# Graph network on one core: node addition, exponentials and node-row copy of two convolutions in units of 1024 columns

## The chip, the core and the metric

The kernel runs on one core of a Trainium2 chip. The metric is the device time of one execution in microseconds (us); lower is better.

## What is computed

Four graph layers follow one another over 50,000 nodes of 128 features and 25,000 edges sorted by destination. Layer 1 holds the two convolutions that are changed here. Cut to one of them (8 heads of 16 channels):

```python
q = (x @ qw + qb).reshape(N, HEADS, CH)      # k and v alike
alpha = jnp.sum(q[dst] * k[src], axis=-1) * SCALE
m = jax.ops.segment_max(alpha, dst, num_segments=N)
a = jnp.exp(alpha - m[dst])
denom = jax.ops.segment_sum(a, dst, num_segments=N)
a = a / denom[dst]
msg = v[src] * a[:, :, None]
out = jax.ops.segment_sum(msg, dst, num_segments=N).reshape(N, HEADS * CH)
return out + x @ sw + sb
```

The first convolution is followed by a relu, the second by the addition of x and a layer norm.

## The kernel before

The work is cut into 49 tiles. A tile is 512 edges and 1024 node rows. Tables lie in HBM: each node has a row, and each run of edges with one destination leaves its result in an edge row; a later layer gathers from both. In `conv` (line 773) features lie on the partitions while edges run along the free dimension.

One step of the loop handles tile `now`, finishes tile `last` (one before) and, in the first convolution, stores what `old` (two before) left. The order on each engine is written out by hand in the four `step` functions; each engine runs its own order, and semaphores alone join them. The loop `run_steps` (line 75) writes out 6 steps, runs a hardware loop of 6 steps a turn, and writes out the rest.

- POOL gathers 4 x 128 source rows and 4 x 128 destination rows a tile (line 765), two tiles of buffers.
- SP loads the 1024 node rows of the tile and stores results.
- TensorE turns source rows (`turn(0)`), destination rows (`turn(1)`), multiplies q, turns both halves of the node rows (`turn(2)`, `turn(3)`), multiplies k and v, then `own_rows(now, 0)` (node rows times the self weight), in the second convolution `own_rows(now, 1)` too, then the sum over heads into `psA`. In the first convolution `own_rows(now, 1)` stands after `psA`. Last come 16 matmuls for the edge rows of `last` into `psE[2]`.
- ScalarE copies the turned rows out of PSUM (lines 946 and 975), keeps q, takes the exponentials `c` of `dropm` and `p` of `u` (lines 960 and 964), and the logarithm and exponential that invert the denominator. In the first convolution it applies the relu to edge and node rows; in the second it makes squares (line 954) and scales rows (line 931).
- VectorE runs the chain over the edges: running maximum `m` (line 1023), `drop`, `u`, `dropm`, then with the exponentials `pv` and the scans `den` and `num`, then `kq` of the current tile, `agg` of the last, and the node addition: line 1077 in the first convolution (adds a bias row), line 1009 in the second (`add_x1`, adds a prepared row). The reduction of squares `c_var` (line 444) stands between `dropm` and `pv` in the second.

PSUM is full: `psT` two banks, `psQ`, `psV`, `psA` one each, `psE` three (two for node rows, one for edge rows). The semaphore `en_ready` counts finished halves of node rows, `pren_ready` their additions, `turned_sb` the copies of turned rows (four a tile).

Of the kernel before, what the change touches and what calls it, by code (L numbers as in the profile page):

```python
# [768 lines left out]
def conv(nc, io, h, layer):  # L769
# [3 lines left out]
    with ExitStack() as ctx:  # L773
# [17 lines left out]
        drop, dropm, c, u, p = (sb(n, [P, TILE]) for n in ("drop", "dropm", "c", "u", "p"))  # L791
# [7 lines left out]
        psT = [bank(f"psT{k}") for k in range(2)]  # L799
        psQ, psV, psA = bank("psQ"), bank("psV"), bank("psA")  # L800
        psE = [bank(f"psE{k}") for k in range(3)]
# [5 lines left out]
         drop_ready, dropm_ready, c_ready, u_ready, p_ready, pv_ready, den_ready, num_ready, lnd_ready, rden_ready,  # L807
# [3 lines left out]
             "carry_ready", "m_ready", "drop_ready", "dropm_ready", "c_ready", "u_ready", "p_ready", "pv_ready",  # L811
# [12 lines left out]
        @block.sync  # L824
        def _(sp):
            def step(t):
                now, last, (g, a, b) = t.tile(0), t.tile(1), t.group(2)
                if now:
                    s = now.slot
                    wait(sp, turned, 4 * now.n - 4)  # L830
                    sp.dma_start(xn[:, s, :, :], node_rows(table, now.n)).then_inc(node_landed[s], 16)
                    if not layer:
                        here = bass.ds(now.n * TILE, TILE)
                        wait(sp, m_ready, now.n - 1)
                        sp.dma_start(h.far[:, here], io["far"][:, here].to_broadcast([P, TILE])
                                     ).then_inc(far_landed[s], 16)
                if layer:

                    u0 = t.group(0)[0]
                    if u0:  # L840

                        wait(sp, pren_ready, 2 * u0.n - 2)
                        sp.sem_inc(starts_sp, 1)
                        wait(sp, pree_ready, u0.n - 2)
                        sp.sem_inc(starts_sp, 1)
                    if now:
                        sp.dma_start(x1r[:, u0.slot, 0:2, :], node_rows(io["x1b"], now.n)).then_inc(x1n_landed[now.slot], 16)
                    if last:
                        sp.dma_start(by_row(x1r[:, u0.slot, 2, :]),
                                     edge_rows(io["x1"], last.n)).then_inc(x1e_landed[last.slot], 16)  # L850
                if layer:
                    store_group(sp, g, a, b, t, result, xo, out_ready, node_stored, edge_stored)
                    return
                if last:
                    sp.wait_ge(out_ready, last.n + 1)
                    sp.dma_start(node_rows(result, last.n), xo[:, last.slot, 0:2, :]).then_inc(node_stored[last.slot], 16)
                old = t.tile(3)
                if old:
                    sp.wait_ge(oute_ready, old.n + 1)
                    sp.dma_start(edge_rows(result, old.n), by_row(xe[:, old.slot, :])).then_inc(edge_stored[old.slot], 16)  # L860

            run_steps(sp, 3, step)
            all_stored(sp, node_stored, edge_stored)

        @block.tensor
        def _(pe):
            def turn(k, now, rows, landed, count):
                pe.wait_ge(landed, count)
                wait(pe, turned_sb, 4 * now.n + k - 1)
                for o, x in zip(quarters(psT[k % 2]), quarters(rows)):  # L870
                    ins = nc.tensor.transpose(o, x, h.w["ident"][:, :])
                ins.then_inc(turned, 1)

            def own_rows(now, k):

                pe.wait_ge(turned_sb, 4 * now.n + 3 + k)
                wait(pe, pren_ready, 2 * now.n - 1 + k)
                for o, x in zip(quarters(psE[k]), quarters(xnT[:, now.slot, k, :])):
                    ins = nc.tensor.matmul(o, x, w_s[:, :], start=True, stop=True)
                ins.then_inc(en_ready, 1)  # L880

            def step(t):
                now, last = t.tile(0), t.tile(1)
                if now:
# [3 lines left out]
                    pe.wait_ge(turned_sb, 4 * now.n + 2)  # L888
# [17 lines left out]
                if last:  # L906
# [3 lines left out]
                    for o, x, y in zip(quarters(psE[2]), quarters(agg), quarters(xdT[:, last.slot, :])):  # L910
# [7 lines left out]
        def _(act):  # L918
# [17 lines left out]
            def step(t):  # L936
                now, last, old, (g, a, b) = t.tile(0), t.tile(1), t.tile(2), t.group(1)
                if now:
                    s = now.slot
                    for k, dst in enumerate((xsT[:, s, :], xdT[:, s, :])):  # L940
# [5 lines left out]
                        nc.scalar.activation(dst, psT[k][:, :], ACT.Copy).then_inc(turned_sb, 1)  # L946
                if layer and g:

                    if a == 0:
                        act.wait_ge(pren_ready, 2 * g.n + 2)  # L950
# [6 lines left out]
                if last:  # L957
                    act.wait_ge(dropm_ready, last.n + 1)
                    wait(act, num_ready, last.n)
                    nc.scalar.activation(c[:, :], dropm[:, :], ACT.Exp).then_inc(c_ready, 1)  # L960
                    act.wait_ge(u_ready, last.n + 1)
                    wait(act, pv_ready, last.n)
                    wait(act, den_ready, last.n)
                    nc.scalar.activation(p[:, :], u[:, :], ACT.Exp).then_inc(p_ready, 1)
                if old and not layer:
                    act.wait_ge(ee_ready, old.n + 1)
                    wait(act, edge_stored[old.slot], 16 * old.half)
                    nc.scalar.activation(xe[:, old.slot, :], psE[2][:, :], ACT.Relu).then_inc(oute_ready, 1)
# [21 lines left out]
                if now and not layer:  # L990
                    act.wait_ge(pren_ready, 2 * now.n + 2)
# [6 lines left out]
        def _(dve):  # L998
            nc.vector.memset(m[:, 0, 0:1], 0.0).then_inc(carry_ready, 1)

            def add_x1(t, g, k):
                now, old = t.tile(0), t.tile(2)
                if k < 2:
                    dve.wait_ge(en_ready, 2 * now.n + 1 + k)
                    dve.wait_ge(x1n_landed[now.slot], 16 * (now.half + 1))
                else:
                    dve.wait_ge(ee_ready, old.n + 1)
                    dve.wait_ge(x1e_landed[old.slot], 16 * (old.half + 1))
                nc.vector.tensor_tensor(pre[:, g.slot, k, :], psE[k][:, :], x1r[:, g.slot, k, :],
                                        ALU.add).then_inc(pren_ready if k < 2 else pree_ready, 1)  # L1010

            def step(t):
# [12 lines left out]
                if layer and b == 3:  # L1025
                    add_x1(t, g, 2)
                if last:
# [4 lines left out]
                    wait(dve, p_ready, last.n)  # L1032
                    nc.vector.tensor_tensor(u[:, :], psA[:, :], m[:, s, 1:TILE + 1], ALU.subtract).then_inc(u_ready, 1)
                    dve.wait_ge(drop_ready, last.n + 1)
                    wait(dve, c_ready, last.n)
# [6 lines left out]
                if last:  # L1042

                    dve.wait_ge(p_ready, last.n + 1)
# [4 lines left out]
                    dve.wait_ge(c_ready, last.n + 1)  # L1049
# [22 lines left out]
                if now and not layer:  # L1072

                    wait(dve, out_ready, now.n - 1)
                    for k in range(2):
                        dve.wait_ge(en_ready, 2 * now.n + 1 + k)
                        nc.vector.tensor_tensor(by_row(pre[:, now.slot, k, :]), by_row(psE[k][:, :]),  # L1077
                                                s_bias[:, :].rearrange("p (o f) -> p o f", o=1).to_broadcast([P, 4, P]),
                                                ALU.add).then_inc(pren_ready, 1)
                if layer:  # L1080
# [4 lines left out]
                    for k in range(a0, min(b0, 2)):  # L1085
                        add_x1(t, g0, k)
# [816 lines left out]
```

## Time and profile before

| | us |
|---|---|
| median of 3 runs | 3386.93 |
| lowest, highest | 3383.4, 3388.3 |
| the profiled execution | 3391.02 |
| its span in the trace | 3389.2 |
| VectorE busy | 2556.6 (75%) |
| TensorE busy (matmuls) | 2705.1 (80%) |
| ScalarE busy | 2020.4 (60%) |
| POOL busy | 2088.8 (62%) |

The span is the trace's own time from first to last instruction. Busy shares are means over stages with different limits. The stages that count here are the first convolution (about 681 to 1243 us) and the second (about 1245 to 1826 us). In the rows further down an idle time in brackets is that of the engine just before the instruction, with what ended it. Tiles carry a prefix in the trace: `c_` is either convolution. `c_psE` there is any of the three banks, and `s_b` and `x1r` are what the node addition adds.

### The profile page before, as it was taken

How to read it: one execution, taken by the hardware profiler on the slowest of the kernel's cores; microseconds unless marked ns; L12 is line 12 of the kernel's file. 1: busy time of each engine (PE TensorE's matmuls, PEld its weight loads, DVE VectorE, ACT ScalarE, POOL GpSimd, SP SyncE). 2: the span in 40 equal slices, each digit the busy share in tenths (PEclk: the TensorE clock that was granted, in tenths of full speed). 3: DMA queues.
4: the chain of work that ended last, by engine and by line, in shares of the span. 5: the costliest groups of instructions: out<-in, count | busy, mean ns of one | idle time of the engine just before them, and what ended most of it. 6: DMA issues, size and time to landing. Idle time of an engine off the chain costs nothing. (4 is left out here: it accounts for less than half of the span.)

```text
span 3389.2 us, 49347 instructions
## 1 busy us (share of the span) xinstructions
PE 2705.1 (80%) x14422; PEld 1818.1 (54%) x14422; DVE 2556.6 (75%) x2973; ACT 2020.4 (60%) x3316; POOL 2088.8 (62%) x1966
## 2 busy tenths in 40 slices
PE   7899999778888868888886899999999875444442
PEld 3466666556666645656563356666666554323221
DVE  6699999958888859999995269989989997323332
ACT  0167777545665548898985577787787775111111
POOL 4477777377777747777773764555554000777776
PEclk9999999989999989999997999999999997666666
DMA  6366676645555547776763266666666563322221
GB/s 204 112 195 218 221 222 219 197 152 179 185 181 177 178 145 225 228 234 226 235 225 113 56 170 183 182 194 182 184 187 191 163 194 126 88 71 75 77 82 40
DMA packets 447965, 569.11 MB, mean 168 GB/s; under 512 B 60559, under 2 KB 253255, under 8 KB 447682
## 3 DMA queue, kind: packets, MB, share of 16 engines
q1 hardware_dynamic: 379758, 441.14, 42.1%
q0 software_dynamic: 62720, 124.71, 13.4%
q10 hardware_dynamic: 5332, 1.32, 0.2%
q8 instruction: 82, 1.34, 0.2%
q14 instruction: 73, 0.60, 0.1%
HBM read 350.28 MB, written 220.55 MB: 168 GB/s over the span
## 5 line engine op out<-in xcount | busy, mean ns | idle before, releaser
L1176 POOL DMA_INDIRECT g_xd_xs<-table_x,dst_row x196 | 230.7, 1177 | 315.9 <-PE g_psT L1241 222.1
L1673 POOL DMA_INDIRECT f_xs<-table_x,src_row x196 | 188.6, 962 | 314.9 <-POOLq L1100 255.5
L765 POOL DMA_INDIRECT c_xs<-table_h,src_row x196 | 215.0, 1097 | 121.0 <-issue 75.9
L506 POOL DMA_INDIRECT xs<-in_x,src_i x196 | 227.4, 1160 | 84.9 <-issue 55.2
L491 POOL DMA_INDIRECT xd<-in_x,dst_i x196 | 217.0, 1107 | 96.6 <-issue 47.2
L1722 PE MATMUL f_psT<-w_ident,f_xs 128*128 128x128 f32 x196 | 53.0, 424 | 277.9 <-DMA f_xs<-table_x,src_row 277.9
L765 POOL DMA_INDIRECT c_xs<-table_x,src_row x196 | 201.6, 1029 | 116.5 <-issue 62.4
L1736 ACT ACTIVATE f_reluT<-f_psY 128x512 f32<-128x512 f32 x49 | 29.3, 597 | 403.9 <-PE f_psY L1715 403.9
L1176 POOL DMA_INDIRECT g_xd_xs<-table_x,src_row x196 | 221.8, 1132 | 59.7 <-issue 59.4
L765 POOL DMA_INDIRECT c_xd<-table_x,dst_row x196 | 204.7, 1044 | 59.7 <-issue 59.7
L1782 DVE TENSOR_TENSOR_SCAN f_red<-f_cont,f_red,f_psT 128x512 f32<-128x512 uint8 x48 | 61.4, 1280 | 226.9 <-PE f_psT L1722 226.8
L1680 POOL DMA_INDIRECT out<-f_xo,end_i x196 | 195.6, 998 | 59.7 <-issue 59.1
L765 POOL DMA_INDIRECT c_xd<-table_h,dst_row x196 | 185.8, 948 | 59.7 <-issue 59.7
L1722 PEld LDWEIGHTS f_psT<-w_ident,f_xs 128*128 128x128 f32 x196 | 34.3, 212 | 344.7 <-DMA f_xs<-table_x,src_row 343.0
L1246 PE MATMUL g_psP<-w_center,g_turns 128*128 128x128 f32 x1568 | 196.8, 279 | 17.4 <-ACT g_turns L1376 11.2
L1246 PEld LDWEIGHTS g_psP<-w_center,g_turns 128*128 128x128 f32 x1568 | 186.9, 194 | 36.2 <-ACT g_turns L1376 14.5
L1463 DVE TENSOR_REDUCE g_var<-g_sq 128x12 f32<-128x1536 f32 x98 | 171.6, 1751 | 25.2 <-ACT g_sq L1420 22.7
L931 ACT ACTIVATE c_xo<-c_pre,c_rstd 128x128 f32<-128x128 f32 x588 | 181.9, 388 | 5.5 <-ACT c_rstd L456 4.8
L890 PE MATMUL c_psQ<-c_xdT,w_q 128*128 128x512 f32 x196 | 112.9, 658 | 74.6 <-ACT c_xdT L946 74.6
L993 ACT ACTIVATE c_xo<-c_pre 128x1024 f32<-128x1024 f32 x49 | 51.9, 1058 | 166.8 <-DVE c_pre L1077 166.8
L894 PE MATMUL c_psQ<-c_xsT,w_k 128*128 128x512 f32 x196 | 111.3, 650 | 36.1 <-ACT c_q L924 36.1
L896 PE MATMUL c_psV<-c_xsT,w_v 128*128 128x512 f32 x196 | 105.1, 618 | 36.3 <-DVE c_pv L1046 36.3
(313 smaller groups left out, 8689.2 us busy)
## 6 DMA issues: line engine op xcount, KB each, us to landing
g_share<-shares SPq DMA_DIRECT2D x196, 192.0 KB
xn<-in_x SPq DMA_DIRECT2D x49, 512.0 KB
table_x<-xo SPq DMA_DIRECT2D x49, 512.0 KB, 3.0
table_x1b<-xb SPq DMA_DIRECT2D x49, 512.0 KB, 5.4
c_xn<-table_x SPq DMA_DIRECT2D x49, 512.0 KB
table_h<-c_xo SPq DMA_DIRECT2D x49, 512.0 KB
c_xn<-table_h SPq DMA_DIRECT2D x49, 512.0 KB
c_x1r<-table_x1b SPq DMA_DIRECT2D x49, 512.0 KB
```

The lines of the kernel that those rows point to most:

```text
L491: pool.indirect_dma_start(out=quarters(h.xd0[:, s, :])[j], out_offset=None, in_=io["x0"], in_offset=edge_index(h.dst_i, n, j)).then_inc(h. ...
L506: pool.indirect_dma_start(out=quarters(h.xs0[:, s, :])[j], out_offset=None, in_=io["x0"], in_offset=edge_index(h.src_i, n, j)).then_inc(h. ...
L765: pool.indirect_dma_start(out=quarters(rows[:, s, :])[j], out_offset=None, in_=table, in_offset=edge_index(columns, now.n, j)).then_inc(la ...
L890: nc.tensor.matmul(psQ[:, :], w_q[:, :], xdT[:, s, :], start=True, stop=True).then_inc(q_ready, 1)
L894: nc.tensor.matmul(psQ[:, :], w_k[:, :], xsT[:, s, :], start=True, stop=True).then_inc(k_ready, 1)
L896: nc.tensor.matmul(psV[:, :], w_v[:, :], xsT[:, s, :], start=True, stop=True).then_inc(v_ready, 1)
L931: ins = nc.scalar.activation(quarters(xo[:, g.slot, j // 4, :])[j % 4], quarters(pre[:, g.slot, j // 4, :])[j % 4], ACT.Copy, scale=rstd[: ...
L1176: pool.indirect_dma_start(out=quarters(xd_xs[:, s, k, :])[j], out_offset=None, in_=table, in_offset=edge_index(columns, now.n, j)).then_in ...
L1246: ins = nc.tensor.matmul(o, x, h.w["center"][:, :], start=True, stop=True)
L1463: nc.vector.tensor_reduce(var[:, :], by_row(sq[:, :, :].rearrange("p b n -> p (b n)")), AX_X, ALU.add).then_inc(ready, 1)
L1673: pool.indirect_dma_start(out=quarters(xs[:, s, :])[j], out_offset=None, in_=table, in_offset=edge_index(h.src_row, now.n, j)).then_inc(sr ...
L1680: pool.indirect_dma_start(out=io["out"], out_offset=edge_index(h.end_i, old.n, j), in_=quarters(xo[:, s, :])[j], in_offset=None, bounds_ch ...
```

## The change

`dropm` and `u` become the two halves of one buffer `args`, `c` and `p` those of `exps`; one exponential of 1024 columns is taken of the whole buffer once both are there. The two banks of `psT` become one tensor of two banks, and one copy moves both halves of the turned node rows. The node rows get a pair of banks `psN` of their own, with `psE` left as the one bank for edge rows; one addition of 1024 columns handles both halves and waits for the second half's matmuls. `en_ready` and `pren_ready` count once a tile, and `turned_sb` three times. The order of instructions on every engine stays otherwise as it was.

```diff
-        drop, dropm, c, u, p = (sb(n, [P, TILE]) for n in ("drop", "dropm", "c", "u", "p"))
+        drop, args, exps = sb("drop", [P, TILE]), sb("args", [P, 2, TILE]), sb("exps", [P, 2, TILE])
+        (dropm, u), (c, p) = ((x[:, 0, :], x[:, 1, :]) for x in (args, exps))
...
-        psT = [bank(f"psT{k}") for k in range(2)]
+        pair = lambda name: ctx.enter_context(nc.psum_tensor(tag + name, [P, 2, TILE], F32))
+        psT, psN = pair("psT"), pair("psN")
         psQ, psV, psA = bank("psQ"), bank("psV"), bank("psA")
-        psE = [bank(f"psE{k}") for k in range(3)]
+        psE = bank("psE")
...
         def _(pe):
             def turn(k, now, rows, landed, count):
                 pe.wait_ge(landed, count)
-                wait(pe, turned_sb, 4 * now.n + k - 1)
-                for o, x in zip(quarters(psT[k % 2]), quarters(rows)):
+                wait(pe, turned_sb, 3 * now.n + max(k - 1, 0))
+                for o, x in zip(quarters(psT[:, k % 2, :]), quarters(rows)):
                     ins = nc.tensor.transpose(o, x, h.w["ident"][:, :])
                 ins.then_inc(turned, 1)
 
             def own_rows(now, k):
 
-                pe.wait_ge(turned_sb, 4 * now.n + 3 + k)
-                wait(pe, pren_ready, 2 * now.n - 1 + k)
-                for o, x in zip(quarters(psE[k]), quarters(xnT[:, now.slot, k, :])):
+                pe.wait_ge(turned_sb, 3 * now.n + 3)
+                wait(pe, pren_ready, now.n)
+                for o, x in zip(quarters(psN[:, k, :]), quarters(xnT[:, now.slot, k, :])):
                     ins = nc.tensor.matmul(o, x, w_s[:, :], start=True, stop=True)
-                ins.then_inc(en_ready, 1)
+                if k == 1:
+                    ins.then_inc(en_ready, 1)
...
                 if last:
                     act.wait_ge(dropm_ready, last.n + 1)
+                    act.wait_ge(u_ready, last.n + 1)
                     wait(act, num_ready, last.n)
-                    nc.scalar.activation(c[:, :], dropm[:, :], ACT.Exp).then_inc(c_ready, 1)
-                    act.wait_ge(u_ready, last.n + 1)
                     wait(act, pv_ready, last.n)
                     wait(act, den_ready, last.n)
-                    nc.scalar.activation(p[:, :], u[:, :], ACT.Exp).then_inc(p_ready, 1)
+                    nc.scalar.activation(exps[:, :, :], args[:, :, :], ACT.Exp).then_inc(exps_ready, 1)
...
                 if now:
                     if not layer:
                         keep_q(now)
-                    for k in range(2):
-                        act.wait_ge(turned, 4 * now.n + k + 3)
-                        wait(act, en_ready, 2 * now.n - 3 + k)
-                        nc.scalar.activation(xnT[:, s, k, :], psT[k][:, :], ACT.Copy).then_inc(turned_sb, 1)
+                    act.wait_ge(turned, 4 * now.n + 4)
+                    wait(act, en_ready, now.n - 1)
+                    nc.scalar.activation(xnT[:, s, :, :], psT[:, :, :], ACT.Copy).then_inc(turned_sb, 1)
...
-            def add_x1(t, g, k):
-                now, old = t.tile(0), t.tile(2)
-                if k < 2:
-                    dve.wait_ge(en_ready, 2 * now.n + 1 + k)
-                    dve.wait_ge(x1n_landed[now.slot], 16 * (now.half + 1))
-                else:
-                    dve.wait_ge(ee_ready, old.n + 1)
-                    dve.wait_ge(x1e_landed[old.slot], 16 * (old.half + 1))
-                nc.vector.tensor_tensor(pre[:, g.slot, k, :], psE[k][:, :], x1r[:, g.slot, k, :],
-                                        ALU.add).then_inc(pren_ready if k < 2 else pree_ready, 1)
+            def add_nodes(now, g):
+                dve.wait_ge(en_ready, now.n + 1)
+                dve.wait_ge(x1n_landed[now.slot], 16 * (now.half + 1))
+                nc.vector.tensor_tensor(pre[:, g.slot, 0:2, :], psN[:, :, :], x1r[:, g.slot, 0:2, :],
+                                        ALU.add).then_inc(pren_ready, 1)
+
+            def add_edges(old, g):
+                dve.wait_ge(ee_ready, old.n + 1)
+                dve.wait_ge(x1e_landed[old.slot], 16 * (old.half + 1))
+                nc.vector.tensor_tensor(pre[:, g.slot, 2, :], psE[:, :], x1r[:, g.slot, 2, :],
+                                        ALU.add).then_inc(pree_ready, 1)
...
                 if now and not layer:
 
                     wait(dve, out_ready, now.n - 1)
-                    for k in range(2):
-                        dve.wait_ge(en_ready, 2 * now.n + 1 + k)
-                        nc.vector.tensor_tensor(by_row(pre[:, now.slot, k, :]), by_row(psE[k][:, :]),
-                                                s_bias[:, :].rearrange("p (o f) -> p o f", o=1).to_broadcast([P, 4, P]),
-                                                ALU.add).then_inc(pren_ready, 1)
+                    dve.wait_ge(en_ready, now.n + 1)
+                    nc.vector.tensor_tensor(by_row(pre[:, now.slot, 0:2, :].rearrange("p b n -> p (b n)")),
+                                            by_row(psN[:, :, :].rearrange("p b n -> p (b n)")),
+                                            s_bias[:, :].rearrange("p (o f) -> p o f", o=1).to_broadcast([P, 8, P]),
+                                            ALU.add).then_inc(pren_ready, 1)
                 if layer:
 
                     g0, a0, b0 = t.group(0)
                     if g0:
                         wait(dve, out_ready, g0.n - 1)
-                    for k in range(a0, min(b0, 2)):
-                        add_x1(t, g0, k)
+                    if g0 and a0 == 0:
+                        add_nodes(now, g0)
```

What is left out renames the same counts and buffers elsewhere (for example `wait(sp, pren_ready, 2 * u0.n - 2)` becomes `u0.n - 1`).

## Rows read from the trace of the kernel before

**Rows 1.** Windows of both convolutions: length, PE, PEld, DVE, ACT, POOL busy, PEclk, DMA.

```profile
720.00:1230.00 510.00, 439.55 (x2614) 323.26 (x2614) 412.01 (x560) 305.70 (x512) 376.79 (x362) 1.00 0.57 177
1280.00:1800.00 520.00, 446.71 (x2555) 312.10 (x2556) 501.49 (x641) 467.40 (x1098) 374.69 (x365) 1.00 0.72 230
```

**Rows 2.** Waits, 680 to 1245 us: waiting work, what ended it, us, times, longest.

```profile
DVE c_pv L1046 <- ACT c_p L964: 56.5, 49, 1.2
...
DVE c_pre L1077 <- PE c_psE L879: 45.9, 50, 1.1
...
PE c_psT L871 <- DMA c_xs<-table_x,src_row: 21.7, 1, 21.7
```

**Rows 3.** Timeline, one step of the first convolution: start us, us, engine, line, operation.

```profile
1010.00 1.27 DVE L1023 TENSOR_TENSOR_SCAN c_m<-far,c_m,c_psA 128x512 f32<-128x512 f32 x1
...
1011.61 0.60 ACT L946 ACTIVATE c_xsT<-c_psT 128x512 f32<-128x512 f32 x1 [0.36 <-PE c_psT L871]
...
1013.23 0.63 ACT L960 ACTIVATE c_c<-c_dropm 128x512 f32<-128x512 f32 x1 [0.53 <-DVE c_dropm L1036]
...
1013.77 0.61 ACT L964 ACTIVATE c_p<-c_u 128x512 f32<-128x512 f32 x1
...
1014.42 0.75 DVE L1046 SCALAR_TENSOR_TENSOR c_pv<-c_psV,b_vs,c_p 128x512 f32<-128x512 f32 x1 [1.15 <-ACT c_p L964]
...
1015.33 1.08 ACT L975 ACTIVATE c_xnT<-c_psT 128x512 f32<-128x512 f32 x2
...
1015.50 1.13 PE L894 MATMUL c_psQ<-c_xsT,w_k 128*128 128x512 f32 x2 [0.74 <-ACT c_q L924]
...
1017.32 1.05 PE L879 MATMUL c_psE<-w_s,c_xnT 128*128 128x128 f32 x8
...
1018.24 1.13 PE L903 MATMUL c_psA<-c_kq,w_heads 128*128 128x512 f32 x2
...
1018.69 0.69 DVE L1077 TENSOR_TENSOR c_pre<-c_psE,s_b 128x512 f32<-128x512 f32 x1
...
1019.20 1.05 PE L879 MATMUL c_psE<-w_s,c_xnT 128*128 128x128 f32 x8
...
1020.29 0.69 DVE L1077 TENSOR_TENSOR c_pre<-c_psE,s_b 128x512 f32<-128x512 f32 x1 [0.91 <-PE c_psE L879]
```

**Rows 4.** Tile c_pre, 670 to 1245 us: min, median, max ns, first and last start.

```profile
L1077 DVE TENSOR_TENSOR c_pre<-c_psE,s_b x98: 681/691/693, 701.7 to 1228.1; 128x512 f32<-128x512 f32 x98
```

**Rows 5.** Waits of the second convolution, 1250 to 1810 us.

```profile
DVE c_var L444 <- ACT c_sq L954: 18.0, 47, 0.4
```

**Rows 6.** Timeline, part of one step of the second convolution.

```profile
1503.48 1.28 DVE L1009 TENSOR_TENSOR c_pre<-c_psE,c_x1r 128x512 f32<-128x512 f32 x2
...
1503.94 0.38 PE L911 MATMUL c_psE<-w_center,c_agg 128*128 128x128 f32 x2
...
1506.37 0.60 ACT L946 ACTIVATE c_xsT<-c_psT 128x512 f32<-128x512 f32 x1 [0.90 <-PE c_psT L871]
...
1508.85 1.75 DVE L444 TENSOR_REDUCE c_var<-c_sq 128x12 f32<-128x1536 f32 x1 [0.37 <-ACT c_sq L954]
...
1509.80 0.64 ACT L964 ACTIVATE c_p<-c_u 128x512 f32<-128x512 f32 x1
...
1510.52 0.74 DVE L1046 SCALAR_TENSOR_TENSOR c_pv<-c_psV,b_vs,c_p 128x512 f32<-128x512 f32 x1
```

**Rows 7.** Groups by form, whole run, at 1024 columns: us, mean ns, idle before.

```profile
L750 DVE TENSOR_TENSOR xb<-xo,s_b1c 128x1024 f32<-128x1024 f32 x49 | 60.0, 1224 | 1.7
L1623 DVE TENSOR_TENSOR g_pre<-g_psP,g_xn 128x1024 f32<-128x1024 f32 x49 | 59.9, 1221 | 21.6 <-PE g_psP L1246 21.6
...
L993 ACT ACTIVATE c_xo<-c_pre 128x1024 f32<-128x1024 f32 x49 | 51.9, 1058 | 166.8 <-DVE c_pre L1077 166.8
...
L662 ACT ACTIVATE nodeT<-psT 128x1024 f32<-128x1024 f32 x49 | 49.8, 1016 | 3.8 <-PE psT L582 3.8
```

**Rows 8.** Line L765, gathers of the first convolution: min, median, max ns.

```profile
L765 POOL DMA_INDIRECT c_xs<-table_x,src_row x196: 940/944/1540, 681.3 to 1203.5; - x196
```

More of the change, by code:

```diff
@@ L840, in step @@
                     if u0:
-                        wait(sp, pren_ready, 2 * u0.n - 2)
+                        wait(sp, pren_ready, u0.n - 1)
                         sp.sem_inc(starts_sp, 1)
@@ L887, in step @@
                     turn(1, now, xd[:, s, :], dst_landed[s], 64 * (now.half + 1))
-                    pe.wait_ge(turned_sb, 4 * now.n + 2)
+                    pe.wait_ge(turned_sb, 3 * now.n + 2)
                     wait(pe, kq_ready, now.n)
@@ L909, in step @@
                     wait(pe, pree_ready if layer else oute_ready, last.n)
-                    for o, x, y in zip(quarters(psE[2]), quarters(agg), quarters(xdT[:, last.slot, :])):
+                    for o, x, y in zip(quarters(psE), quarters(agg), quarters(xdT[:, last.slot, :])):
                         nc.tensor.matmul(o, x, to_rows[:, :], start=True, stop=False)
@@ L945, in step @@
                             wait(act, ee_ready, now.n - 1)
-                        nc.scalar.activation(dst, psT[k][:, :], ACT.Copy).then_inc(turned_sb, 1)
+                        nc.scalar.activation(dst, psT[:, k, :], ACT.Copy).then_inc(turned_sb, 1)
                 if layer and g:
                     if a == 0:
-                        act.wait_ge(pren_ready, 2 * g.n + 2)
+                        act.wait_ge(pren_ready, g.n + 1)
                     if b == 3:
@@ L990, in step @@
                 if now and not layer:
-                    act.wait_ge(pren_ready, 2 * now.n + 2)
+                    act.wait_ge(pren_ready, now.n + 1)
                     wait(act, node_stored[s], 16 * now.half)
@@ L1025, in step @@
                 if layer and b == 3:
-                    add_x1(t, g, 2)
+                    add_edges(t.tile(2), g)
                 if last:
@@ L1031, in step @@
                                             ALU.subtract).then_inc(drop_ready, 1)
-                    wait(dve, p_ready, last.n)
+                    wait(dve, exps_ready, last.n)
                     nc.vector.tensor_tensor(u[:, :], psA[:, :], m[:, s, 1:TILE + 1], ALU.subtract).then_inc(u_ready, 1)
                     dve.wait_ge(drop_ready, last.n + 1)
-                    wait(dve, c_ready, last.n)
+                    wait(dve, exps_ready, last.n)
                     nc.vector.scalar_tensor_tensor(out=dropm[:, :], in0=drop[:, :], scalar=0.0, in1=h.far[:, here],
@@ L1042, in step @@
                 if last:
-                    dve.wait_ge(p_ready, last.n + 1)
+                    dve.wait_ge(exps_ready, last.n + 1)
                     wait(dve, num_ready, last.n)
```

8 lines of the change are left out of this document (4 added, 4 removed).

## The prediction

> **What bounds the kernel now.** The change touches the two convolutions only, so I read the stage windows first. Over 510 us of the first convolution and 520 us of the second TensorE holds its full granted clock (1.00). VectorE is busy 412 of 510 us (81%) in the first and 501 of 520 us (96%) in the second [rows 1]. In the first no engine is full, so a chain of waits must set the step; in the second VectorE looks like the bound and has to be checked for a wait that comes back in each step.
>
> Waits of the first convolution [rows 2]: VectorE waits 49 times for the second exponential (c_p, 56.5 us, 1.15 us each) and 50 times for the matmuls of the node rows (45.9 us, 0.92 us each). TensorE waited for gathered rows once (21.7 us, the fill). So neither gathers nor VectorE's own load sets the step.
>
> One step in time order [rows 3]: running maximum c_m at 1010.00; the first exponential starts at 1013.23, as soon as dropm is there (ScalarE idle 0.53 before it); the second at 1013.77; pv at 1014.42 after VectorE had waited 1.15; K on TensorE at 1015.50, which waited for q; own rows 0 at 1017.32; psA, which needs kq, at 1018.24; first half of the node addition at 1018.69; matmuls of the second half of the node rows at 1019.20 (TensorE goes straight on from psA to them); second half of the addition at 1020.29, after VectorE had waited 0.91. The next c_m stands behind this addition on VectorE. That closes the cycle: c_m, exponentials, pv, kq, psA, own rows 1, second addition, next c_m. Its length over the stage: the 98 additions start between 701.7 and 1228.1 [rows 4]; taking off the 1.60 from first to second half of one tile (1018.69 to 1020.29), 48 steps take 524.8 us, 10.93 each.
>
> The second convolution [rows 5, 6]: VectorE waits in 47 steps of 49 for the squares c_sq (18.0 us, 0.38 each). The cycle there is kq, psA, the edge rows on TensorE (1503.94 on), the turns of xs, c_xsT (1506.37, ScalarE idle 0.90 before it, until those turns), c_xdT, c_sq, c_var on VectorE (1508.85, idle 0.37 before it), pv, the scans, kq. The two node additions (1503.48, 1.28 us the pair) stand after agg and before c_m, which belongs to VectorE's other branch (c_m, drop, u, dropm): beside that cycle, not on it. That branch has 0.37 us of slack.
>
> **The change, part by part.**
>
> *Node addition, first convolution.* Removed: two instructions of 0.69 us [rows 4]. Added: one of 1024 columns. Two existing instructions bracket it: an addition of 1024 columns from two PSUM banks is 1.221 us, one with the same kind of 8-fold broadcast from SBUF is 1.224 us [rows 7]. I take 1.22. In time on the engine that saves 1.28 - 1.22 = 0.06. But the first half is not on the path: it runs at 1018.69 to 1019.38, in time that VectorE would otherwise spend waiting for the matmuls of 1019.20 [rows 3]. The new addition waits for both halves (en_ready is now raised only by the second), so all 1.22 us come after those matmuls instead of 0.69. Neighbours on VectorE overlap by about 0.1 (the pair of [rows 6] takes 1.28 for twice 0.69), which I take as the same behind a wide one, so c_m starts 1.22 - 0.69 = 0.53 us later. The cover that hid half one is given up. Per tile +0.53, 49 tiles: +26.0 us. What is queued behind the waiting addition is c_m of the next step and all of VectorE's chain; nothing there can go ahead. ScalarE's relu of the node rows, which already waited for both halves, also comes 0.5 later; behind it c_xsT had 0.36 of idle time and c had 0.53 against a c_m that moves as well [rows 3], so it starts nothing late. SP's store of those rows moves with it and has a step of time.
>
> *Exponential, first convolution.* The first one waits for dropm already, and u is made before dropm, so the single one starts when the first did. The pair takes 1013.23 to 1013.77 + 0.61 = 1.15 us. ScalarE's 1024-column relu from SBUF is 1.058 us [rows 7]. I take 1.06 for the exponential, so it saves 0.09. Bounds: 1.06 if it prices like the relu, and at most 1.15 if nothing overlapped away is gained; below 1.06 nothing is excluded by a row, and 1.02 is the price of the 1024-column copy from PSUM [rows 7]: a saving between 0 and 0.13. Both branches behind it (pv on VectorE; xe, q, K on TensorE) move by it together, so it is on the path: -0.09 x 49 = -4.4 us. Scan den needs c, which would be ready later than before, but den stands behind pv, which needs p: no loss.
>
> *Copy of turned node rows, first convolution.* The pair takes 1015.33 to 1016.41 (1.08); one copy of 1024 columns from two banks is 1.016 us [rows 3, 7]. Own rows 0 used to need the first copy only and now need the joint one, done by 1016.4. TensorE is at K and V from 1015.50 on and comes to own rows 0 at 1017.32 [rows 3]. So 0.9 us of cover is left: 0. If that cover were gone it would cost half a copy, 0.5 us a step. The turns of the next tile wait for the joint copy of this one, over at 1016.4; the c_xsT made from them starts at 1011.61 + 10.93 = 1022.5: 0.
>
> First convolution: +0.53 - 0.09 = +0.44 us a step (step 10.93 to 11.37), 49 steps: +21.6 us.
>
> *Second convolution.* Here both halves of own rows are done before psA, so the joint addition waits for nothing new. It saves 1.28 - 1.22 = 0.06 us of VectorE between agg and c_m. That lies beside the binding cycle, and the wait for c_sq grows from 0.37 to about 0.43: worth 0. The joint exponential and copy shorten ScalarE by 0.09 and 0.07, between q and lnv. Their consumer pv starts behind c_var on VectorE, and lnv behind c_var too: 0. Bounds: if the saving of the addition were on the path, -0.06 x 49 = -3 us; if the exponential's were as well, -7 us; p was over at 1509.80 + 0.64 = 1510.44 and pv started at 1510.52 behind c_var, so the exponential was just in time and comes 0.09 sooner now. I take 0.
>
> In the first convolution VectorE is 81% busy and half one runs beside own rows 1 [rows 1, 3]; in the second VectorE is 96% busy. The Trainium skill ("Perfetto Trace Analysis", Optimizing Scalar/DVE Operations) says that grouping helps a saturated engine, while for an unsaturated one that leaves bubbles on others "breaking up instructions may allow work to be completed sooner". By its first half the sum would be that of rival A, by its second a loss in the first convolution, as computed; the trace of the first stage agrees with the second half.
>
> **Sum.** The profiled execution took 3391.0 us, 3391.0 + 21.6 = 3412.6. It lies 4.1 above the median of the runs, 3386.9; a shift of the median by the same 21.6 gives 3408.5 us, which I predict. Own range of this case: the addition between 1.22 and 1.28 (what the pair takes now, start to end), the exponential's saving between 0 and 0.13, the second convolution between -7 and 0: 21.6 + 2.9 + 4.4 = 28.9 above, 21.6 - 2.0 - 7.4 = 12.2 below, so 3399.1 to 3415.8.
>
> **Rivals.**
>
> *A. VectorE's and ScalarE's own work is the bound, and fewer instructions win.* If own rows 1 were finished when agg ends, the joint addition would start at once and everything saved would count: 0.06 + 0.09 in both convolutions, 98 x 0.15 = -14.7 us, 3372.2 us. For it: VectorE is 96% busy in the second convolution. Against it: the wait of 0.91 for own rows 1 in all steps of the first. It decides there: as long as own rows 1 end more than 0.06 after half one could, the joint form loses. Chance 0.07.
>
> *B. The gathers pace the convolutions.* A gather of POOL takes 0.944 us at the median and up to 1.54 [rows 8], and POOL issues them with hardly any pause. If the step of 10.9 us were POOL's, the 0.44 would be taken out of waits and the time stays: 3387. Against it: TensorE waited for gathered rows only in the fill [rows 2], and 8 gathers at the median of 0.944 are 7.6 of the 10.9 us. Chance 0.05.
>
> *C. TensorE loses its clock.* The longer step thins TensorE's work in the first convolution from 86% [rows 1] to about 83%. If the grant fell to its lower level there, K, V, own rows 0, psA and own rows 1 (1015.50 to 1020.2, 4.7 us of each step) would take twice as long: for a tenth of the steps +23 us on top, 3432. Full clock held at 86% in both stages; the trace of before does not show these stages at 83%. Chance 0.05.
>
> *D. The change does not do what it says*, one joint instruction costing as much as two because the two banks are read apart: the addition would be 1.38, 0.16 x 49 = +7.8 us more, 3416. The 1024-column rows from two banks exclude it nearly [rows 7]. Chance 0.02, inside the range.
>
> **How the numbers follow.** Forecast 0.81; A 0.07, B 0.05, C 0.05, D 0.02. The range 3399 to 3417 holds the forecast and D, and leaves out A, B and C. A measurement of this kernel tells about 0.2% (6.8 us) from no change. Slower by more: forecast, C, D, with a little taken off for a forecast case that meets all of its lower bounds: 0.87. Same: B and that little, 0.06. Faster: A, 0.07.
>
> **What would show it.** In the first convolution one c_pre of 128x1024 x49 at about 1.22 us with 1.5 us of idle time before each (75 us in all, against 45.9), c_m starting 1.1 to 1.15 after it, the wait of pv down from 1.15 to 1.06, second additions 11.34 us apart, and the stage ending some 21 us later. In the second: steps still 11.35 apart and the wait for c_sq up from 0.37 to 0.43. The forecast is wrong if the joint addition starts before 10.2 us after c_m, if steps of the first convolution stay under 11.1 us, or if the second's become shorter by over 0.05.

## The result

| | us |
|---|---|
| before, median of 5 runs | 3386.93 (3383.4 to 3388.3) |
| changed, median of 5 runs | 3414.19 (3406.83 to 3415.38) |
| ratio | 1.0077, 95% interval 1.0066 to 1.0089 |
| changed, the profiled execution | 3406.83, span 3405.0 |

The change is slower by 27 us (22 to 30 by the interval). The profiled execution is the fastest of the five, so the loss is placed stage by stage from the two traces. The table gives the starts of the running maximum c_m of the first and last tile of each convolution, and what lies around them:

| stage | before | changed | difference |
|---|---|---|---|
| start to first c_m | 704.1 | 700.5 | -3.6 |
| first convolution, 48 steps | 524.6 | 547.3 | +22.7 |
| between | 38.6 | 38.8 | +0.2 |
| second convolution, 48 steps | 544.5 | 544.3 | -0.2 |
| last c_m to end | 1577.4 | 1574.1 | -3.3 |
| span | 3389.2 | 3405.0 | +15.8 |

In these two executions the change cost 22.7 us, all in the first convolution. The two outer stages together are 6.9 us shorter in the changed kernel's execution, so the spans differ by 15.8 us only. They vary by as much over the six profiles taken at this speed: the first c_m starts at 700.5 to 704.1 us, and the run ends 1573.9 to 1578.5 us after the last one. The other four executions of the changed kernel took 3413.56 to 3415.38 us. None of them was profiled, so it is likely but not shown that their further 7 us, and with them the gap between 22.7 and 27, lie in the outer stages. A kernel of the experiments has such a spread by itself: of five executions of `wide_add_only_2` three took 3409.63 to 3411.05 us and two 3418.46 and 3419.15 us.

### The profile page after: what moved, and what is told of

Its sections match the earlier page's. It is cut to its first block and busy times, and to the rows that moved or that the text cites. A ratio compares the mean times of both kernels' runs of the same rounds, so it can differ in the third digit from the quotient of the medians.

```text
span 3405.0 us, 48520 instructions
## 1 busy us (share of the span) xinstructions
PE 2696.7 (79%) x14422; PEld 1812.1 (53%) x14422; DVE 2547.6 (75%) x2875; ACT 2000.6 (59%) x3120; POOL 2059.6 (60%) x1966
## 5 line engine op out<-in xcount | busy, mean ns | idle before, releaser
L765 POOL DMA_INDIRECT c_xs<-table_x,src_row x196 | 192.6, 982 | 163.8 <-issue 56.2
L765 POOL DMA_INDIRECT c_xs<-table_h,src_row x196 | 215.3, 1099 | 124.4 <-issue 76.2
L506 POOL DMA_INDIRECT xs<-in_x,src_i x196 | 225.8, 1152 | 85.2 <-issue 55.5
L765 POOL DMA_INDIRECT c_xd<-table_h,dst_row x196 | 185.4, 946 | 59.7 <-issue 59.7
L765 POOL DMA_INDIRECT c_xd<-table_x,dst_row x196 | 185.1, 944 | 59.7 <-issue 59.7
L1248 PEld LDWEIGHTS g_psP<-w_center,g_turns 128*128 128x128 f32 x1568 | 184.8, 192 | 36.8 <-ACT g_turns L1378 15.8
L897 PE MATMUL c_psQ<-c_xsT,w_k 128*128 128x512 f32 x196 | 110.9, 648 | 55.5 <-ACT c_q L927 55.5
L966 ACT ACTIVATE c_exps<-c_args 128x1024 f32<-128x1024 f32 x98 | 103.9, 1061 | 52.6 <-DVE c_args L1038 52.5
```

Of the source, the lines that this page charges most:

```text
L506: pool.indirect_dma_start(out=quarters(h.xs0[:, s, :])[j], out_offset=None, in_=io["x0"], in_offset=edge_index(h.src_i, n, j)).then_inc(h. ...
L765: pool.indirect_dma_start(out=quarters(rows[:, s, :])[j], out_offset=None, in_=table, in_offset=edge_index(columns, now.n, j)).then_inc(la ...
L897: nc.tensor.matmul(psQ[:, :], w_k[:, :], xsT[:, s, :], start=True, stop=True).then_inc(k_ready, 1)
L966: nc.scalar.activation(exps[:, :, :], args[:, :, :], ACT.Exp).then_inc(exps_ready, 1)
L1248: ins = nc.tensor.matmul(o, x, h.w["center"][:, :], start=True, stop=True)
```

## The profile after

Waits of the changed kernel, 680 to 1270 us (waiting work, what ended it, us in total, times, longest), answering to [rows 2]:

```profile
DVE c_pre L1078 <- PE c_psN L881: 78.6, 49, 2.7
...
PE c_psQ L897 <- ACT c_q L927: 55.5, 48, 1.2
POOL c_xs L765 <- PE c_psT L873: 54.4, 34, 1.6
...
DVE c_pv L1048 <- ACT c_exps L966: 52.0, 49, 1.1
```

VectorE now waits 78.6 us for the own rows where it was 45.9, 1.60 a step, and 52.0 instead of 56.5 for the exponential. TensorE waits for q 1.2 us a step (55.5 us in all, 36.1 before): its work did not grow, the step did. POOL, which before ran without a pause, now waits 34 times until a buffer of gathered rows has been turned: with longer steps the gathers run into their buffers. So they do not set the changed kernel's step. That they did not set the step of 10.9 us before either is shown by `rows_early_2` below, where the same gathers keep up with steps of 10.42 us.

One step as in [rows 3], start us, us, engine, line, operation:

```profile
1005.98 1.05 PE L881 MATMUL c_psN<-w_s,c_xnT 128*128 128x128 f32 x8
...
1007.14 1.23 DVE L1078 TENSOR_TENSOR c_pre<-c_psN,s_b 128x1024 f32<-128x1024 f32 x1 [1.58 <-PE c_psN L881]
...
1008.28 1.27 DVE L1025 TENSOR_TENSOR_SCAN c_m<-far,c_m,c_psA 128x512 f32<-128x512 f32 x1
...
1011.51 1.06 ACT L966 ACTIVATE c_exps<-c_args 128x1024 f32<-128x1024 f32 x1 [1.08 <-DVE c_args L1038]
...
1012.60 0.75 DVE L1048 SCALAR_TENSOR_TENSOR c_pv<-c_psV,b_vs,c_exps 128x512 f32<-128x512 f32 x1 [1.06 <-ACT c_exps L966]
...
1013.69 1.12 PE L897 MATMUL c_psQ<-c_xsT,w_k 128*128 128x512 f32 x2 [1.21 <-ACT c_q L927]
...
1015.51 1.05 PE L881 MATMUL c_psN<-w_s,c_xnT 128*128 128x128 f32 x8
...
1016.42 1.13 PE L906 MATMUL c_psA<-c_kq,w_heads 128*128 128x512 f32 x2
...
1017.39 1.05 PE L881 MATMUL c_psN<-w_s,c_xnT 128*128 128x128 f32 x8
...
1018.55 1.23 DVE L1078 TENSOR_TENSOR c_pre<-c_psN,s_b 128x1024 f32<-128x1024 f32 x1 [1.58 <-PE c_psN L881]
...
1019.69 1.27 DVE L1025 TENSOR_TENSOR_SCAN c_m<-far,c_m,c_psA 128x512 f32<-128x512 f32 x1
```

From c_m to c_m are 11.41 us. Own rows 1 starts 9.11 after c_m (before 9.20: the exponential's gain). But c_m follows 2.30 us after the start of own rows 1 (1017.39 to 1019.69), where it was 1.09 to the second addition and 0.6 more. Half one, which ran beside own rows 1 at 1018.69 in [rows 3], is now in the 1.23 us at 1018.55, behind them.

The wide additions of both convolutions by tile (min, median, max ns), answering to [rows 4], and the exponential from the page:

```profile
L1078 DVE TENSOR_TENSOR c_pre<-c_psN,s_b x49: 1224/1225/1225, 699.3 to 1246.7; 128x1024 f32<-128x1024 f32 x49
L1005 DVE TENSOR_TENSOR c_pre<-c_psN,c_x1r x49: 1208/1217/1225, 1285.5 to 1829.8; 128x1024 f32<-128x1024 f32 x49
```

```profile
L966 ACT ACTIVATE c_exps<-c_args 128x1024 f32<-128x1024 f32 x98 | 103.9, 1061 | 52.6 <-DVE c_args L1038 52.5
```

1.225 and 1.061 us: the prices taken from [rows 7]. The second convolution: four more lines of the step of before in [rows 6], then a step of the changed kernel, then its waits:

```profile
1502.87 0.69 DVE L1071 TENSOR_TENSOR c_agg<-c_num,c_rden 128x512 f32<-128x512 f32 x1
...
1504.68 1.27 DVE L1023 TENSOR_TENSOR_SCAN c_m<-far,c_m,c_psA 128x512 f32<-128x512 f32 x1
...
1505.51 0.39 PE L912 MATMUL c_psE<-s1c,c_xdT 128*128 128x128 f32 x2
...
1505.93 0.69 DVE L1009 TENSOR_TENSOR c_pre<-c_psE,c_x1r 128x512 f32<-128x512 f32 x1
```

```profile
1522.02 0.68 DVE L1073 TENSOR_TENSOR c_agg<-c_num,c_rden 128x512 f32<-128x512 f32 x1
...
1522.62 1.22 DVE L1005 TENSOR_TENSOR c_pre<-c_psN,c_x1r 128x1024 f32<-128x1024 f32 x1
...
1523.75 1.27 DVE L1025 TENSOR_TENSOR_SCAN c_m<-far,c_m,c_psA 128x512 f32<-128x512 f32 x1
...
1524.68 0.39 PE L915 MATMUL c_psE<-s1c,c_xdT 128*128 128x128 f32 x2
...
1525.10 0.69 DVE L1011 TENSOR_TENSOR c_pre<-c_psE,c_x1r 128x512 f32<-128x512 f32 x1
...
1528.03 1.75 DVE L444 TENSOR_REDUCE c_var<-c_sq 128x12 f32<-128x1536 f32 x1 [0.38 <-ACT c_sq L957]
```

```profile
DVE c_var L444 <- ACT c_sq L957: 18.0, 47, 0.4
...
DVE c_pre L1011 <- PE c_psE L915: 1.3, 7, 0.2
```

c_m follows agg by 1.73 us instead of 1.81 (1.74 and 1.80 at the median of all steps), so the wide form saves 0.06 to 0.08. The edge addition behind c_m now starts 1.35 after it (before 1.25 here, 1.28 at the median). In both kernels it starts 0.03 us after the modelled end of TensorE's edge rows (1505.90 and 1525.07), and seven waits for them are on record in the changed kernel, none in the same steps before. So TensorE holds the edge addition, which starts as long after agg as before, 3.1 us. The wait for c_sq stays at 18.0 us in 47 steps.

## The experiments

Twelve runs on three chips. On two of them, called disturbed below (first eight runs), the kernels took 3736 to 3779 us, the one before 3745 and 3742, and steps of the first convolution ran from 10 to 17 us; on the third (last four, "at full clock") all was as in the first profiles. So of the first eight the shortest steps speak, and the times only roughly. Stages at full clock are compared with the first profile of before; no profile of before was taken beside these runs.

**Undo the wide addition in the first convolution alone.**

```diff
-                    dve.wait_ge(en_ready, now.n + 1)
-                    nc.vector.tensor_tensor(by_row(pre[:, now.slot, 0:2, :].rearrange("p b n -> p (b n)")),
...
+                    for k in range(2):
+                        dve.wait_ge(en_ready, 2 * now.n + 1 + k)
+                        nc.vector.tensor_tensor(by_row(pre[:, now.slot, k, :]), by_row(psN[:, k, :]),
...
```

> The changed kernel with the node addition of the first convolution taken apart again: two additions of 512 columns, each waiting for its own half of own rows; the joint exponential, the joint copy and the wide addition of the second convolution stay. Theory (the wide addition lies wholly behind own rows 1, where half of it used to be covered): the step of the first convolution falls from 11.40 to 10.81 us (10.90 of before less 0.09 of the exponential), the time is 4 us under before, 3383, and 31 under the changed kernel. Rival (the joint exponential or the joint copy holds the chain up): the step stays above 11.0 and the time above 3395. Rival (the pairing of PSUM banks itself costs): the same, above 3395, with the wait for own rows unchanged at 1.6 us.

> The changed kernel with the node addition of the first convolution in two again, a second time. On the chip of the first time transfers were slower and most steps had other waits; the undisturbed ones took 10.80 us. Theory: where transfers are as fast as in the profile of before, all steps take 10.81, and the time is 4 us under before, 3383. Rival (joint exponential or copy costs): not under before.

> The changed kernel with the node addition of the first convolution in two, a third time, for a chip on which TensorE keeps its full clock through the first convolution, as in the profiles of before and after. Theory: all steps there take 10.81 us and the time is 4 us under before (ratio 0.9988). Rival (the joint exponential or copy costs): ratio 1.002 or more. If the clock falls in spells again, only the shortest steps speak: 10.80.

First and second: 3744.3 and 3743.9 against 3745.3 and 3742.1 us of before, ratios 1.0012 (0.9992 to 1.0031) and 1.0003 (0.9987 to 1.0018), shortest steps 10.80. Third: 3381.2 against 3388.7, ratio 0.9981 (0.9971 to 0.9990), 7.6 us less where 4 were expected; first convolution 520.3 us, 4.3 less than before, median step 10.81. Own rows 1 and what follows, in that kernel:

```profile
1001.72 0.68 DVE L1079 TENSOR_TENSOR c_pre<-c_psN,s_b 128x512 f32<-128x512 f32 x1
...
1002.21 1.05 PE L881 MATMUL c_psN<-w_s,c_xnT 128*128 128x128 f32 x8
...
1003.31 0.69 DVE L1079 TENSOR_TENSOR c_pre<-c_psN,s_b 128x512 f32<-128x512 f32 x1 [0.91 <-PE c_psN L881]
...
1003.91 1.27 DVE L1025 TENSOR_TENSOR_SCAN c_m<-far,c_m,c_psA 128x512 f32<-128x512 f32 x1
```

Half one is back beside own rows 1, and c_m follows own rows 1 by 1.70 us instead of 2.30. All of the loss goes with the wide addition of the first convolution, and the rest of the change is a small gain. PSUM pairing costs nothing: psN is a pair here too.

**One edit at a time.** `exps_only` is the kernel before with the joint exponential; `wide_add_only` the changed kernel with exponential and copy in two:

```diff
-                    nc.scalar.activation(exps[:, :, :], args[:, :, :], ACT.Exp).then_inc(exps_ready, 1)
+                    nc.scalar.activation(c, dropm, ACT.Exp).then_inc(exps_ready, 1)
...
+                    nc.scalar.activation(p, u, ACT.Exp).then_inc(exps_ready, 1)
```

> The kernel before with the joint exponential alone. Theory: the exponential pair of 1.15 us becomes one of 1.06 on the path of the first convolution, step 10.90 to 10.81, time 4.3 us less, 3382.6; nothing in the second convolution, where pv stands behind c_var. Rival (scan den or q waits longer since c comes later): step 10.90 or more, time 3387 or more. Rival (ScalarE's work bounds the second convolution): its step falls from 11.35 to 11.26, time 9 us less, 3378.

> The changed kernel with exponential and copy taken apart again, so that the wide node addition (both convolutions) is the only edit. Theory: own rows 1 to c_m takes 2.30 instead of 1.70 us in the first convolution, step 10.90 to 11.50, 49 steps, time 29 us more than before, 3416; second convolution unchanged at 11.35. Rival (the joint copy is part of the loss, since own rows 0 wait for it): here the loss is smaller than in the changed kernel, under 24 us, 3410 or less.

> The wide node addition as the only edit, a second time. Its shortest steps were 11.50 us. Theory: at full clock all steps of the first convolution take 11.50, the time is 29 us over before (ratio 1.0085) and 4 over the changed kernel. If the clock falls in spells again: shortest steps 11.50, ratio near 1.010 as the first time.

The exponential alone: ratio 1.0016 (0.9998 to 1.0034) on a disturbed chip, shortest step 10.80 as the theory has it; its time at full clock was not measured. The wide addition alone: 1.0100 (1.0073 to 1.0126), then 1.0071 (1.0057 to 1.0085), 3411.1 against 3388.7 us, 22 us where 29 were expected. Its stage says otherwise: 551.7 us, 27.1 over before, median step 11.50. The medians take in what the outer stages do; the profiled execution is one of the two slower ones, and its span, 3416.6, is 27.4 over the 3389.2 of before. Its waits, 680 to 1245 us:

```profile
DVE c_pre L1080 <- PE c_psN L881: 76.9, 48, 2.7
...
DVE c_pv L1050 <- ACT c_exps L967: 54.2, 47, 1.2
```

Step 11.50 here, 11.40 with exponential and copy joined: 0.10 for these two, as 10.90 to 10.81 above.

**The changed kernel again.**

> The changed kernel unaltered, for a second profile and more times. The first convolution was 22.7 us longer than before in the first profile, the second 0.2 shorter, and the stages that the change does not touch 6.9 us shorter. Theory (the untouched stages differ from run to run): again 547 us for the first convolution, 544 for the second, and untouched stages 3 to 8 us longer than in the first profile, so that the time is near 3414. Rival (the change lengthens an untouched stage in most executions): the start of the first convolution or what follows the second is longer than in the profile of before by 3 us or more.

3770.7 against 3745.3 us, ratio 1.0079 (1.0054 to 1.0104), shortest steps 11.40. It ran on a disturbed chip, so its stages cannot be set beside the first profiles. Against the rival that the change lengthens an outer stage stand the profiles at full clock: with the wide addition these stages take together 2274.6 us (changed), 2281.8 (`wide_add_only_2`) and 2274.7 (`rows_early_2`), before 2281.5. Where the slower executions of the changed kernel spend their further 7 us stays open.

**Own rows 1 ahead of psA**, so that it isn't the last thing of a step:

```diff
-                    if layer:
-                        own_rows(now, 1)
+                    own_rows(now, 1)
...
-                    if not layer:
-                        own_rows(now, 1)
```

> The changed kernel with own rows 1 of the first convolution put ahead of psA on TensorE, as it stands in the second convolution. Theory (the wide addition costs only because it waits for own rows 1 as the last thing of the step): own rows 1 ends 0.9 us earlier after c_m, the wait of 1.58 us before the addition falls to about 0.6, undisturbed steps of the first convolution take 10.45 us instead of 11.40, and the time is some 22 us under before and 46 under the changed kernel. Rival (the wide form is slower in itself): steps stay over 10.9. Rival (psA, now 0.9 later, holds up c_m instead): the step is near 10.9, with VectorE waiting for c_psA.

> The changed kernel with own rows 1 ahead of psA in the first convolution, a second time. Shortest steps were 10.42 us. Theory at full clock: steps 10.42 or as near to it as the gathers allow (8 at 1.25 us and what VectorE holds up), time 17 to 23 us under before (ratio 0.994). Rival: the gathers hold the steps at 10.9, ratio 1.000. If the clock falls in spells again: ratio 1.000 as the first time.

> The kernel before with own rows 1 of the first convolution ahead of psA. Theory: half one of the addition follows agg without a wait, half two ends before psA does, and c_m waits for psA: steps of 10.3 us where undisturbed instead of 10.90, time 29 us under before. Rival (gathers set a floor of 10.9): the steps stay at 10.9 with TensorE waiting for gathered rows.

First: ratio 1.0007 (0.9988 to 1.0027), shortest step 10.42. Second, at full clock: 3361.3 against 3388.7 us, ratio 0.9924 (0.9910 to 0.9937), 27 us under before where 17 to 23 were expected; all steps but the first (9.86) 10.41 to 10.43. In that kernel:

```profile
1009.64 1.95 PE L881 MATMUL c_psN<-w_s,c_xnT 128*128 128x128 f32 x16
...
1010.41 0.68 DVE L1070 TENSOR_TENSOR c_agg<-c_num,c_rden 128x512 f32<-128x512 f32 x1
...
1011.42 1.02 PE L905 MATMUL c_psA<-c_kq,w_heads 128*128 128x512 f32 x2
1011.69 1.22 DVE L1075 TENSOR_TENSOR c_pre<-c_psN,s_b 128x1024 f32<-128x1024 f32 x1 [0.60 <-PE c_psN L881]
...
1012.83 1.27 DVE L1022 TENSOR_TENSOR_SCAN c_m<-far,c_m,c_psA 128x512 f32<-128x512 f32 x1
```

The same wide addition waits 0.6 us instead of 1.58. psA and the addition now run side by side, and c_m starts 1.41 us after psA, where it takes 1.39 when it waits for psA alone (`add_later_2` below): both are ready at nearly the same time. This beats both kernels; the gain is in the first convolution, 499.7 us against 524.6. TensorE waits for gathered rows only in the fill, so gathers don't set this step. The kernel before with the same move (ratio 0.9989, 0.9974 to 1.0004, disturbed chip) had two steps of 10.17 and 10.28, where the theory had 10.3, and no other under 10.8; the first is 0.25 under the wide form. Whether it is faster at full clock was not measured.

**The wide addition inside VectorE's wait for the exponential.** The addition of `last` goes between the copy of the carry and pv of the next step, its relu behind the reciprocal, its store a step later:

```diff
                     nc.vector.tensor_copy(m[:, 1 - s, 0:1], m[:, s, TILE:TILE + 1]).then_inc(carry_ready, 1)
+                if last and not layer:
+                    wait(dve, out_ready, last.n - 1)
+                    dve.wait_ge(en_ready, last.n + 1)
+                    nc.vector.tensor_tensor(by_row(pre[:, last.slot, 0:2, :].rearrange("p b n -> p (b n)")),
...
```

> The changed kernel with the wide node addition of the first convolution moved on VectorE from the end of a step to the next one, between the copy of the carry and pv, where VectorE waits 1.06 us for the exponential; the relu of the node rows follows the reciprocal on ScalarE, and SP stores them one step later, so that the next load is not queued behind the store. Theory (the addition is worth its time only where the engine waits anyway): c_m starts as soon as psA is there, undisturbed steps would be 9.5 us, and the gathers, 8 at 1.25 us, hold them at 10.0 to 10.4; time 24 to 44 us under before. Rival (the gathers, which VectorE holds up for 0.9 us a step, set 10.9): no better than the split addition. Rival (the addition delays pv by more than 0.1 us): steps over 10.4 with VectorE never waiting for the exponential.

> The changed kernel with the wide addition moved into VectorE's wait for the exponential, a second time. Shortest steps were 9.96 us, the pace of 8 gathers. Theory at full clock: steps of 10.0 to 10.4, time 24 to 44 us under before (ratio 0.987 to 0.993). Rival: the gathers, held up by VectorE, hold the steps at 10.9, ratio 1.000. If the clock falls in spells again: ratio 0.998 as the first time.

First: ratio 0.9984 (0.9969 to 1.0000). Second: 3367.9 against 3388.7 us, ratio 0.9936 (0.9922 to 0.9950); 21 us, a little short of the 24 to 44 expected; median step 10.44, from 9.20 (the first, with rows gathered ahead) to 12.56.

```profile
1003.79 1.28 DVE L1026 TENSOR_TENSOR_SCAN c_m<-far,c_m,c_psA 128x512 f32<-128x512 f32 x1 [0.85 <-PE c_psA L907]
...
1006.75 0.60 ACT L950 ACTIVATE c_xsT<-c_psT 128x512 f32<-128x512 f32 x1 [3.91 <-PE c_psT L874]
...
1006.90 0.66 PE L874 MATMUL c_psT<-w_ident,c_xd 128*128 128x128 f32 x4 [0.27 <-DMA c_xd<-table_x,dst_row]
...
1006.98 1.21 DVE L1046 TENSOR_TENSOR c_pre<-c_psN,s_b 128x1024 f32<-128x1024 f32 x1
...
1007.59 0.60 ACT L950 ACTIVATE c_xdT<-c_psT 128x512 f32<-128x512 f32 x1 [0.24 <-PE c_psT L874]
1008.09 1.05 ACT L967 ACTIVATE c_exps<-c_args 128x1024 f32<-128x1024 f32 x1
...
1009.17 0.75 DVE L1056 SCALAR_TENSOR_TENSOR c_pv<-c_psV,b_vs,c_exps 128x512 f32<-128x512 f32 x1 [0.98 <-ACT c_exps L967]
```

c_m waits for psA only. The addition fits in front of pv, which still waits 0.98 us for the exponential. That one started at 1008.09, a microsecond after its input, because ScalarE takes it behind the copies of the turned rows (1006.75 and 1007.59), and these wait for TensorE. TensorE comes to its turns behind own rows 1 and the edge rows; in this step the gathered destination rows hold it up for 0.27 us more, over the stage 24 times for 17.7 us in all. So with VectorE's cover used well, two things hold the step: the place of the turns on TensorE, and the gathers. Which of them weighs more was not tried.

## Why the prediction held, and what was off

*Place and sign of the loss.* Right. The wide addition waits for own rows 1 and takes half one with it; undoing it alone took the loss away, doing it alone brought it back, and moving own rows 1 forward turned the loss into a gain.

*Size of the addition.* Predicted +0.53 a step, measured +0.60 at the median step (11.50 against 10.90) and 0.59 (11.40 against 10.81). The term that was short is "c_m starts 1.22 - 0.69 = 0.53 us later". The duration was right (1.225), and so was the overlap behind it: c_m starts 1.14 us after the wide addition and 0.61 after the narrow one. But the wide addition also starts 1.16 us after own rows 1 does, the narrow one 1.09, in the changed kernel against before and split_add_3. Over 48 steps these 0.07 us are 3.4 us. It goes with the wide form, not with the pair of banks; why a wide addition starts later was not tried.

*Longer steps of before.* By the whole stages the wide addition costs less than 48 times 0.60: 27.1 us (551.7 against 524.6) and 27.0 (547.3 against 520.3), 0.56 a step. The prediction took all steps of before as equal (10.93, the mean). In fact they are 10.9 us, but for twelve, two in each six, of 10.97 to 11.10 us, together 1.7 us. `split_add_3` has the same pattern, the kernels with the wide addition do not. Six steps are a turn of the hardware loop; what lengthens these steps was not tried.

*Exponential.* Predicted -0.09 a step, measured -0.09 to -0.10 with the copy.

*Copy of node rows.* Costed at nothing. No run isolates it; own rows 0 keeps its place (7.23 us after c_m, 7.32 before, with the exponential's 0.09), so the joint copy didn't hold it up.

*Second convolution.* Total right, 0 (-0.2 us). The reason was off by one step: "the wait for c_sq grows from 0.37 to about 0.43" did not happen. The 0.06 to 0.08 us saved ahead of c_m are lost at the edge addition, which starts only when TensorE's edge rows are there and which stands ahead of c_var on VectorE; so VectorE came to its wait for c_sq no sooner than before.

*The sum.* 48 steps were to cost 21.1 us and cost 22.7: 28.8 for the addition, less 4.4 for exponential and copy, less 1.7 for the longer steps of before. That it came so near is in part luck, since the later start (+3.4) and the longer steps (-1.7) were both left out and pull apart. The time was forecast as 3408.5 us and is 3414.2, inside the range. Of the 27.3 us between the medians 4.6 lie outside these 22.7, and where is not shown (see the result).

*Rivals.* A (fewer instructions win) fell: some 0.15 us of engine time a step was saved and the kernel is slower. By the Trainium skill ("VectorE: DVE Perf Modes", The TRN2 errata) an fp32 tensor_tensor of N columns takes (N + 151) cycles at 0.96 GHz, 0.691 us at 512; worked out from it, an estimate for 1024 is 1.224. The trace agrees (0.691, 1.225). Of the 0.16 us between two additions of 0.691 and one of 1.225 the overlap of neighbours had already hidden 0.1. B (gathers pace the stage) fell: POOL waits for buffers now, and steps went down to 10.42. Further on, in `add_later_2`, TensorE does wait for gathered rows in half of the steps. C (clock) did not happen in the changed kernel on the first chip: granted clock 1.00 at 429 of 520 us busy, 83% as forecast. D fell with 1.225 us.

## What to carry to other kernels

Before two instructions become one, look at what each of the two waits for. If the first ran in time that the engine spends waiting for the second's input, joining them moves its whole duration onto the path, and that costs more than the saved overhead gives back (0.6 us against under 0.1 here). The joint form does no harm where both inputs are there early, as in the second convolution. Elsewhere move the producer up (0.9924 here) or the consumer into another wait of its engine (0.9936), and judge by which wait ends last in the step. Neither run shows that the joint form itself helps: with the producer moved up, the shortest step was 10.17 us with two halves and 10.42 with the joint form, on a disturbed chip.

## What the runs showed of the hardware

Two chips ran every kernel some 10% longer. One kernel on two chips (split_add_2, split_add_3), windows of the first convolution (length; PE, PEld, DVE, ACT, POOL busy; PEclk; DMA share; GB/s), and from the first a step:

```profile
800.00:1300.00 500.00, 399.43 (x2150) 290.70 (x2150) 344.63 (x464) 246.45 (x349) 314.41 (x310) 0.90 0.50 153
```

```profile
720.00:1210.00 490.00, 425.72 (x2537) 313.29 (x2536) 398.18 (x542) 289.70 (x405) 371.00 (x360) 1.00 0.59 181
```

```profile
1237.71 1.05 PE L881 MATMUL c_psN<-w_s,c_xnT 128*128 128x128 f32 x8
...
1240.86 0.69 DVE L1079 TENSOR_TENSOR c_pre<-c_psN,s_b 128x512 f32<-128x512 f32 x1 [2.89 <-remote]
```

Two stretches of 5 us of `split_add_2`, the first with this own rows 1, the second shortly behind it:

```profile
1235.00:1240.00 5.00, 5.00 (x34) 3.94 (x33) 2.08 (x4) 1.61 (x3) 3.78 (x5) 1.00 0.21 54
...
1245.00:1250.00 5.00, 4.97 (x12) 3.12 (x13) 3.12 (x3) 3.24 (x5) 3.98 (x4) 0.50 0.89 225
```

The granted clock falls from 1.00 to a mean of 0.90, with spells at the lower level of 1.2 GHz (0.50 in the second stretch). The change is not the cause: over whole runs the kernel before has 0.87 to 0.89 on these two chips and 0.91 to 0.93 on the third. The recorded duration of a VectorE addition is the same, 0.69 us, but it starts 3.15 us after own rows 1 instead of 1.09, though it waits for nothing else (the profile names what ended its wait only as `remote`): what TensorE computes comes late to the others, later than the modelled ends of the matmuls show, and in this step in a stretch granted 1.00. The expectation of `split_add_2` blamed slower transfers; the windows above do not bear that out, 153 GB/s at a busy share of 0.50 and 181 at 0.59 are the same rate while busy. On such a chip a step holds other waits, and the differences between these kernels shrink (0.9924 becomes 1.0007) or stay (1.0079). Why the clock falls there, and why results come late, is open.
